# DLRM tower: the last tile in two halves, the layers of the tile before it sooner, and the ids loaded first

## The reference

```
e = jnp.stack([tbl_0[ids[:, 0]], ..., tbl_31[ids[:, 31]]], axis=1)        # [2048, 32, 256]
dots = jnp.einsum('bnd,bmd->bnm', x, x);  z = dots[:, iu, ju]              # pairs i < j, 496 of them
h = jnp.concatenate([z, dense_ctx], axis=1)                                # [2048, 512]
h = jnp.maximum(h @ W_top1 + b_top1, 0.0)                                  # 512
h = jnp.maximum(h @ W_top2 + b_top2, 0.0)                                  # 256
y = h @ W_top3                                                             # [2048, 1]
```

## Time and profile before

| | |
|---|---|
| median of 3 runs | 615.87 us (612.99 to 616.21) |
| the profiled execution | 614.14 us, its span 612.3 us |
| PE, share of the span busy | 85% |
| POOL | 71% |
| DVE, ACT | 45%, 34% |

### The profile page before, as it was taken

The page is one execution under the profiler, slowest core; times in us unless marked ns, Lnnn a source line. Parts: engine busy times, 40 slices in busy tenths (PEclk is TensorE's granted clock), DMA queues, the critical chain, the costliest instruction groups (busy, mean ns, idle before and its releaser), DMA issues.

```text
span 612.3 us, 24786 instructions
## 1 busy us (share of the span) xinstructions
PE 522.7 (85%) x11392; PEld 466.6 (76%) x11392; DVE 278.3 (45%) x600; ACT 209.6 (34%) x390; POOL 432.1 (71%) x463
## 2 busy tenths in 40 slices
PE   1068998999999999988999898989989897996967
PEld 0054796998889897978889786978878796984857
DVE  0013744827364545555273535556263555426060
ACT  1044233343433334343334224333332333432130
POOL 6767677777777777777777777777777777777600
PEclk9978998999999999998999999999999999998788
DMA  5695443443434343433434343434434333333300
GB/s 155 210 241 191 136 139 107 110 126 107 122 111 125 109 121 112 125 107 108 124 110 123 106 126 111 122 107 112 125 105 122 109 109 108 107 108 111 97 3 1
DMA packets 26411, 72.10 MB, mean 118 GB/s; under 512 B 8426, under 2 KB 9338, under 8 KB 25680
## 3 DMA queue, kind: packets, MB, share of 16 engines
q0 software_dynamic: 21888, 59.80, 35.5%
q1 hardware_dynamic: 4420, 10.72, 5.6%
HBM read 70.48 MB, written 0.01 MB: 115 GB/s over the span
## 4 chain that ended last, share of the span: by engine, by line
PE 65%; DMA 14%; POOL 11%; issue 7%; ACT 1%; DVE 1%; SPq 0%; POOLq 0%; ACTq 0%
PE ps_l L268 18%; PE ps_turn L205 15%; POOL rows L192 11%; PE ps_gram L252 11%; DMA rows<-in_table,index 10%; PE ps_pick L234 7%; PE ps_pick L236 7%; DMA pick_id<-in_pick_ids 5%; PE ps_l L279 2%; PE ps_l L220 1%; PE ps_pick L220 1%; PE ps_l L286 1%; DVE pairs L422 0%; PE ps_l L222 0%; PE ps_pick L222 0%
## 5 line engine op out<-in xcount | busy, mean ns | idle before, releaser
L192 POOL DMA_INDIRECT rows<-in_table,index x456 | 431.2, 946 | 146.3 <-issue 118.8
L422 DVE COPY pairs<-ps_gram 32x112 f32<-32x112 f32 (+1 forms) x504 | 189.1, 375 | 140.9 <-PE ps_gram L252 134.5
L327 ACT COPY cols<-ps_turn 128x512 f32<-128x512 f32 x228 | 132.1, 590 | 314.5 <-PE ps_turn L205 314.1
L205 PE MATMUL ps_turn<-identity,rows 128*128 128x128 f32 x912 | 148.2, 293 | 59.0 <-DMA rows<-in_table,index 44.6
L205 PEld LDWEIGHTS ps_turn<-identity,rows 128*128 128x128 f32 x912 | 104.0, 147 | 74.8 <-DMA rows<-in_table,index 41.2
L252 PE MATMUL ps_gram<-cols 128*32 128x32 f32 x8192 | 113.5, 201 | 22.9 <-issue 21.3
L252 PEld LDWEIGHTS ps_gram<-cols 128*32 128x32 f32 x8192 | 93.4, 111 | 49.9 <-issue 44.4
L410 DVE TENSOR_TENSOR one_hot<-ps_ids,row_number 125x2048 fp32r<-125x2048 f32 x28 | 63.9, 2281 | 139.5 <-ACT ps_ids L339 118.9
L268 PE MATMUL ps_l<-pairs,w_sb 128*128 128x128 f32 x1024 | 121.9, 282 | 3.1 <-DVE score L441 3.1
L268 PEld LDWEIGHTS ps_l<-pairs,w_sb 128*128 128x128 f32 x1024 | 120.5, 199 | 3.6 <-DVE pairs L422 3.6
L234 PE MATMUL ps_pick<-one_hot,table_hi 125*128 125x256 f32 x448 | 115.1, 295 | 0.4 <-ACT stage L343 0.4
(11 more groups left out here) (31 smaller groups left out, 79.1 us busy)
## 6 DMA issues: line engine op xcount, KB each, us to landing
rows<-in_table,index POOLq DMA_INDIRECT x456
pick_id<-in_pick_ids SPq DMA_DIRECT2D x14, 250.0 KB
w_sb<-in_w_t SPq DMA_DIRECT2D x1, 2048.0 KB, 29.9
cols<-in_tbl SPq DMA_DIRECT2D x2, 1000.0 KB
stage<-in_tbl SPq DMA_DIRECT2D x2, 1000.0 KB
w_sb<-in_W_top SPq DMA_DIRECT2D x1, 512.0 KB, 32.6
pairs<-in_dense_t SPq DMA_DIRECT2D x16, 8.0 KB
scores<-score SPq DMA_DIRECT2D x16, 0.5 KB
```

Source lines behind the costliest of these rows:

```text
L192: pool.indirect_dma_start(out=rows[x % ROWS][:, k, :], out_offset=None, in_=table, in_offset=bass.IndirectOffsetOnAxis(ap=index[:, t, SUBS ...
L205: last = pe.transpose(ps_turn[x % TURNS][:, h, SPG * k:SPG * (k + 1), :], rows[x % ROWS][:, k, h * P:(h + 1) * P], identity[:, :])
L327: act.copy(cols[t % COLS][:, :, :, FPU * u:FPU * (u + 1)], ps_turn[x % TURNS][:, :, :, :]).then_inc(cols_ready, 1)
L422: last = dve.tensor_copy(pairs[n % 2][N_FIELDS * q:N_FIELDS * (q + 1), c0:KC, TQ * j + FQ * u:TQ * j + FQ * (u + 1)] .rearrange("p c g -> ...
```

## The change

- The ids of the first two picks are loaded ahead of the first two tables.
- In the last two blocks of the loop, t = 30 and 31, `gram_parts` has two parts, at u = 0 and u = 1.
- Tile 14: `layer1` moves from block 31, u = 1 to block 30, u = 5; `relu1` to block 31, u = 0; `layer2` from behind the loop to block 31, u = 2; `layer3` from behind `gram(31)` to block 31, u = 5. Its layers 2 and 3 write the bank of the picks (`ps_late`, a view of `ps_pick`) instead of `ps_l1`. `layer3(13)` moves from u = 4 to u = 2 of block 30.
- Tile 15 is split in halves. Its first half, the 64 samples of block 30, runs `layer1` in block 31 (`first_half_layer1(0)` at u = 4 and `(2)` at u = 5: 32 matmuls of 128 columns of weights by 64 moving columns) and `layer2` right behind `gram(31)`. Its second half, the samples of block 31, runs layers 1 and 2 "column-tiled": each matmul of 128 output rows becomes four of 32, one for each column group of the array, 128 matmuls in layer 1 and 32 in layer 2, 64 moving columns each. The rectifying of the second half's layer 1 is shared by ACT and DVE. Layer 3 and the score run once over all 128 samples.

```diff
...
     def gram_parts(t):
+        if t >= BLOCKS - 2:
+            return {0: (0, FQ // 2), 1: (FQ // 2, FQ)}
         return {2: (0, 4), 3: (4, 8), 4: (8, 12), 5: (12, 16)} if t % 2 == 1 else {1: (0, 6), 2: (6, 11), 3: (11, 16)}

...
+        ps_late = ps_pick[:, :, :].rearrange("p h s -> p (h s)")
+        ps_late_l2 = [ps_late[:, P * m:P * (m + 1)] for m in range(M2C)]
+        ps_late_l3 = ps_late[0:1, 2 * P:3 * P]
+        ps_last_l1 = [ps_l1[:, 0, :], ps_l1[:, 1, :], ps_ids[:, 0:P], ps_ids[:, P:2 * P]]
+        ps_last_l3 = ps_late[0:1, 3 * P:4 * P]
...
+            load_ids(0)
+            load_ids(1)
             load_table(0)
             load_table(1)
-            load_ids(0)
-            load_ids(1)
...
-                if n == TILES - 1:
-                    pe.wait_ge(last_pairs_ready, 1)
...
+                if n == TILES - 2:
...
+                        last = pe.matmul(ps_late_l2[m] if n == TILES - 2 else ps_l1[:, m, :], w2_sb[:, c, m * P:(m + 1) * P],
...
+                    last = pe.matmul(ps_late_l3 if n == TILES - 2 else ps_l1[0:1, M2C, :], w3_sb[:, m:m + 1],
...
+            def last_pairs(c, half):
+                return pairs[(TILES - 1) % 2][:, c, :].rearrange("p (j u g) -> p j u g", j=QUAD, u=2)[:, :, half, :]
+
+            def first_half_layer1(m0):
+                if m0 == 0:
+                    pe.wait_ge(pairs_ready, BLOCKS - 1)
+                    pe.wait_ge(dense_loaded[(TILES - 1) % 2], 16 * TILES // 2)
+                    pe.wait_ge(hidden1_ready, TILES - 1)
+                for m in range(m0, m0 + 2):
+                    for c in range(KC):
+                        last = pe.matmul(ps_last_l1[m][:, 0:BLOCK], w1_sb[:, c, m * P:(m + 1) * P], last_pairs(c, 0),
+                                         start=(c == 0), stop=(c == KC - 1))
+                if m0 == 2:
+                    last.then_inc(l1_done, 1)
...
+            def first_half_layer2():
...
+                for m in range(M2C):
+                    for c in range(M1C):
+                        last = pe.matmul(ps_late_l2[m][:, 0:BLOCK], w2_sb[:, c, m * P:(m + 1) * P],
+                                         hidden1[:, c, 0:BLOCK], start=(c == 0), stop=(c == M1C - 1))
...
+            def second_half_layer1():
+                pe.wait_ge(pairs_ready, BLOCKS)
+                pe.wait_ge(last_pairs_ready, 1)
+                for m in range(M1C):
+                    for c in range(KC):
+                        for j in range(QUAD):
+                            p0 = N_FIELDS * j
+                            last = pe.matmul(ps_last_l1[m][p0:p0 + N_FIELDS, BLOCK:P],
+                                             w1_sb[:, c, m * P + p0:m * P + p0 + N_FIELDS], last_pairs(c, 1),
+                                             start=(c == 0), stop=(c == KC - 1))
+                last.then_inc(l1_done, 1)
+
+            def second_half_layer2():
+                pe.wait_ge(last_hidden1_ready, 2)
+                pe.wait_ge(hidden2_ready, TILES)
...
+                            last = pe.matmul(ps_late_l2[m][p0:p0 + N_FIELDS, BLOCK:P],
+                                             w2_sb[:, c, m * P + p0:m * P + p0 + N_FIELDS], hidden1[:, c, BLOCK:P],
+                                             start=(c == 0), stop=(c == M1C - 1))
+                last.then_inc(l2_done, 1)
...
+            def last_layer3():
...
+                    last = pe.matmul(ps_last_l3, w3_sb[:, m:m + 1], hidden2[:, m, :],
...
-                    if t >= 3 and t % 2 == 1 and u == 1:
+                    if 3 <= t < BLOCKS - 1 and t % 2 == 1 and u == 1:
...
-                    if t >= 4 and t % 2 == 0 and u == 4:
+                    if t >= 4 and t % 2 == 0 and u == (2 if t == BLOCKS - 2 else 4):
...
-            layer2(TILES - 2)
+                    if t == BLOCKS - 2 and u == 5:
+                        layer1(TILES - 2)
+                    if t == BLOCKS - 1 and u == 2:
+                        layer2(TILES - 2)
+                    if t == BLOCKS - 1 and u == 4:
+                        first_half_layer1(0)
+                    if t == BLOCKS - 1 and u == 5:
+                        layer3(TILES - 2)
+                        first_half_layer1(2)
             gram(BLOCKS - 1, 0, FQ)
-            layer3(TILES - 2)
-            layer1(TILES - 1)
-            layer2(TILES - 1)
-            layer3(TILES - 1)
+            first_half_layer2()
+            second_half_layer1()
+            second_half_layer2()
+            last_layer3()
...
-                    if t >= 3 and t % 2 == 1 and u == 3:
+                    if 3 <= t < BLOCKS - 1 and t % 2 == 1 and u == 3:
                         relu1((t - 3) // 2)
+                    if t == BLOCKS - 1 and u == 0:
+                        relu1(TILES - 2)
...
+            act.wait_ge(l1_done, TILES)
+            act.wait_ge(l2_done, TILES - 1)
+            for m in range(M1C):
+                rectified = act.activation(hidden1[:, m, 0:BLOCK], ps_last_l1[m][:, 0:BLOCK], ACT.Relu,
+                                           bias=b1_sb[:, m:m + 1])
+            rectified.then_inc(hidden1_ready, 1)
...
-            relu1(last)
+            act.wait_ge(l1_done, TILES + 1)
+            for m in range(2):
+                rectified = act.activation(hidden1[:, m, BLOCK:P], ps_last_l1[m][:, BLOCK:P], ACT.Relu,
+                                           bias=b1_sb[:, m:m + 1])
+            rectified.then_inc(last_hidden1_ready, 1)
...
+            def relu2_half(half):
+                dve.wait_ge(l2_done, TILES + half)
+                for m in range(M2C):
+                    last = dve.tensor_scalar(hidden2[:, m, BLOCK * half:BLOCK * (half + 1)],
+                                             ps_late_l2[m][:, BLOCK * half:BLOCK * (half + 1)], b2_sb[:, m:m + 1],
+                                             0.0, ALU.add, ALU.max)
+                last.then_inc(hidden2_ready, 1)
...
+                if t % 2 == 0 and 4 <= t < BLOCKS:
                     take_score((t - 4) // 2)
+                if t == BLOCKS - 1:
+                    relu2(TILES - 2)
+                    take_score(TILES - 2)
                 if t % 2 == 0 and t < JOBS:
                     make_one_hot(t)
-            relu2(TILES - 1)
-            take_score(TILES - 1)
+            relu2_half(0)
+            dve.wait_ge(l1_done, TILES + 1)
+            for m in range(2, M1C):
+                last = dve.tensor_scalar(hidden1[:, m, BLOCK:P], ps_last_l1[m][:, BLOCK:P], b1_sb[:, m:m + 1],
+                                         0.0, ALU.add, ALU.max)
+            last.then_inc(last_hidden1_ready, 1)
+            relu2_half(1)
+            dve.wait_ge(l3_done, TILES)
+            dve.wait_ge(stored[(TILES - 1) % 2], 16 * (TILES // 2 - 1))
+            dve.tensor_copy(score[:, (TILES - 1) % 2, :].rearrange("p (j u g) -> p j u g", j=QUAD, u=2),
+                            ps_last_l3.rearrange("p (u j g) -> p j u g", u=2, j=QUAD)).then_inc(score_ready, 1)
...
```

More of the change, by code:

```diff
@@ L285, in layer3 @@
                 for m in range(M2C):
-                    last = pe.matmul(ps_l1[0:1, M2C, :], w3_sb[:, m:m + 1], hidden2[:, m, :],
+                    last = pe.matmul(ps_late_l3 if n == TILES - 2 else ps_l1[0:1, M2C, :], w3_sb[:, m:m + 1],
+                                     hidden2[:, m, :], start=(m == 0), stop=(m == M2C - 1))
+                last.then_inc(l3_done, 1)
+            def last_pairs(c, half):
+                return pairs[(TILES - 1) % 2][:, c, :].rearrange("p (j u g) -> p j u g", j=QUAD, u=2)[:, :, half, :]
@@ new lines, in first_half_layer2 @@
+            def first_half_layer2():
+                pe.wait_ge(hidden1_ready, TILES)
+                pe.wait_ge(score_ready, TILES - 1)
+                for m in range(M2C):
[14 more added lines that the diff above has]
+                last.then_inc(l1_done, 1)
@@ L287, in layer3 @@
+            def last_layer3():
+                pe.wait_ge(hidden2_ready, TILES + 1)
+                for m in range(M2C):
+                    last = pe.matmul(ps_last_l3, w3_sb[:, m:m + 1], hidden2[:, m, :],
                                      start=(m == 0), stop=(m == M2C - 1))
@@ L432, in relu2 @@
                 for m in range(M2C):
-                    last = dve.tensor_scalar(hidden2[:, m, :], ps_l1[:, m, :], b2_sb[:, m:m + 1],
+                    last = dve.tensor_scalar(hidden2[:, m, :], ps_late_l2[m] if n == TILES - 2 else ps_l1[:, m, :], b2_sb[:, m:m + 1],
                                              0.0, ALU.add, ALU.max)
@@ L440, in take_score @@
                     dve.wait_ge(stored[n % 2], 16 * (n // 2))
-                dve.tensor_copy(score[:, n % 2, :], ps_l1[0:1, M2C, :]).then_inc(score_ready, 1)
+                dve.tensor_copy(score[:, n % 2, :], ps_late_l3 if n == TILES - 2 else ps_l1[0:1, M2C, :]
+                                ).then_inc(score_ready, 1)
+            def relu2_half(half):
+                dve.wait_ge(l2_done, TILES + half)
+                for m in range(M2C):
```

(4 more changed lines are left out.)

6 lines of the change are left out of this document (3 added, 3 removed).

## The result

The changed kernel takes 623.42 us (median of 4 runs, 620.12 to 624.65), the kernel before beside it 616.04 us (4 runs, 612.99 to 616.29): a ratio of 1.0129 on record, 95% interval 1.0095 to 1.0163 (the two medians divided give 1.0120). The prediction was 611.5 us, range 606.5 to 615.5, with a chance of 0.08 for slower. It was wrong. The profiled execution's span is 621.2 us, 8.9 longer than before.

What follows compares the result with a forecast made beforehand. POOL paces the middle, a serial chain the end. Start -1.8, start of `gram(31)` +5.9, `gram(31)` -1.2, layer 1 -4.9, layer 2 and small steps -1.8: span 608.45 us, predicted time 611.5, range 606.5 to 615.5.

Steps and rivals of the forecast that it cites:

- The clock term of the first half's layer 1: Lower clock after some 3 us of idle PE adds 1.4 us to that layer's 7.3, bounds 0 and 7.3.
- a clock loss that stays: Rival: lower clock through all of both halves' layer 1 (+5.9, +2.3), 619.7 us; chance 0.05.
- Start: Loading the ids first removes POOL's wait near 33 us: -1.8 us, bounds 0 and 2.1.
- the start gives nothing: Rival: POOL's two later waits grow by what the first one lost, 613.3 us; chance 0.22.
- Up to the first half's layer 1: Tile 14's layer 1, then block 30's dot products and copies, end at 582.3 us, where the first half starts.
- Units and layer 3 between its parts: Two transposes, layer 3 of tile 14 and the last unit's evacuation, ahead of block 31's dot products: 2.0 us together.
- `gram(31)`: The dot products of block 31 take 3.7 us instead of 4.9, bounds 2.8 and 4.9.
- Second half's layer 1: At the end, 256 column-tiled records in groups of four take 5.0 us where 9.92 stood.
- The rest of the end: Around the second half's layer 1: copies 3.43 us and a handover, rectifying 0.6, layer 2 1.4, then the small steps.
- The order's loss: Block 31's dot products start 5.9 us later: 7.3 us of layer 1 stand ahead, only half finding idle time.

Runs made afterwards that it cites:

- e8: The kernel before, with layer 1 of tiles 2 to 15 streaming only 64 of its 128 moving columns: 624.39 us, ratio 1.015.
- e1: The changed kernel, with the first half's layer 1 streaming 128 moving columns instead of 64: 617.6 us, ratio 1.0058.
- e7: The kernel before, with layer 1 of the last tile alone streaming only 64 of its 128 moving columns: 621.74 us, ratio 1.0105.
- e9: The kernel before, with the ids of the picks loaded ahead of the small tables: 613.63 us, ratio 0.9989.
- e3: The changed kernel with the last tile undivided, its layers 1 to 3 run whole behind the last dot products: 614.38 us, ratio 1.0.
- e5: e3 with layer 3 of tile 14 behind the last dot products and tile 15's layer 1 not waiting for tile 14's score: 611.86 us, ratio 0.9945.
- e4: e3 with the tables loaded first and 16 unread matmuls between the last dot products and layer 1 of tile 15: 614.05 us, ratio 0.9984.
- e6: e5 with 12 unread matmuls in PE's wait for the last copies: 608.12 us, ratio 0.9879.
- e11: e6 with 22 more unread matmuls in block 30, ahead of layer 1 of tile 14: 612.14 us, ratio 0.9961.

## Why the prediction was wrong, step by step

Against the forecast's 608.45 us of span stand 621.2:

- *The clock term of the first half's layer 1* failed. I took 7.3 + 1.4 us, with 7.3 as the upper bound of the second term; it was 14.2, so 6.9: +5.5. I had seen that half the moving columns don't shorten the record (e8: 7.26 us for 64), and had put the bound right, but sized the term by how layer 1 of tile 14 recovers, which streams 128. e1 and e7 show that this doesn't carry over to 64. This is the rival that had 0.05, "a clock loss that stays": it priced the dot products at 598.9 and the time at 619.7, with the start's 1.8 still in it. But its reason, the wait ahead of the layer, isn't the one that the runs show: e1 has the same wait, and there the clock comes back.
- *Start*: -1.8 forecast, nothing came in this execution: +1.8. The rival "the start gives nothing" is the nearer one (0.2 us over all traces, see e9), but 1.8 isn't excluded by the times.
- *Up to the first half's layer 1*: it starts at 584.39 instead of 582.3: +2.1. The pieces were near (copies of block 29 from 555.87, layer 1 of tile 14 at 562.38 and in 9.71, copies of 6.06), 0.5 and 0.3 later; the other 1.3 are the transposes and dot products of block 30, 6.2 us instead of 4.9, with a stall of 0.82 in "issue".
- *Units and layer 3 between its parts*: 3.2 us instead of 2.0, since they ran at the low clock as well: +1.2.
- *`gram(31)`*: 5.1 us instead of 3.7, just beyond the upper bound of 4.9: +1.4. The stall (1.36) was there, and the records ran partly at the low clock.
- *Second half's layer 1*: 5.9 instead of 5.0, inside the bounds: +0.9. The rest of the end: -0.3 in rectifying and layer 2, +0.1 in the copies.

Together 12.7, from 608.45 to 621.2. The order's loss, `gram(31)` later because 7.3 us of layer 1 stand ahead of it, was forecast at 5.9 and is in e1 594.15 - 587.11 = 7.0; with the low clock it is 14.7. e3 and e5 show that layer 3 of tile 14 ahead of the last dot products (in e3 together with the wait for its score) takes back some 0.55%, e1 against e3 that the halves as placed cost about as much again. That the useful part of the change is the earlier place of tile 14's layers is what then remains of e5's gain; it wasn't tested apart from the two-part dot products.

The chance was sized badly too. The argument against that rival was a row of 128-column records, and no row of before had a record with 64 moving columns; a term with bounds of 0 and 7.3 us, argued from a row of another shape, deserved more than 0.05.

## What to carry to other kernels

Before you shorten the moving operand of a matmul behind a wait, ask for the clock: if the weight load sets the record's time, the narrow record saves nothing and may hold PE at the lower clock (14.2 us instead of 9.3 or 10.6 here). Work split off the end must fill a wait behind the last dependency, not stand ahead of it. And a wait of some 3 us ahead of a long serial matmul stretch is worth filling with matmuls that nobody reads, as long as they end before the wait does (e4's overran it by 0.8 us, and its ratio is 0.9984 where e3 has 1.0): e6 is 1.2% faster than before for that and for the new order of tile 14 with layer 3 behind the dot products.

## What the runs showed of the hardware that I had not expected

- PE busy without a gap for 13.9 us (e7) and the granted clock at 0.50 to its end, while records of the same weights with 128 moving columns raise it within some 5 us. The Trainium skill ("TensorE: Matmul & The Clock Gate", Part 1) says that the clock returns once the engine has been busy. By that rule e7's layer 1 would have taken the 9.92 us of before; it took 13.89, so a PE that the profile shows as busy was not enough here.
- The stalls in "issue" inside the dot products come in every variant, in those of block 31 1.1 us (e3) to 2.6 us (e9) each, and in e11 twice, with 128 records (256 instructions) between them. The profile of the changed kernel has 92 packets for 1.51 MB of instructions, 16 KB each:

```profile
q8 instruction: 92, 1.51, 1.0%
```

In the traces of the kernel before, the changed one and e11, one such packet moves shortly ahead of each of these stalls: 588.0 to 588.5 before the one at 588.7 (kernel before), 603.5 to 604.0 before 605.0 (changed kernel), 584.5 to 585.0 and 588.0 to 588.5 before 585.4 and 588.4 (e11). That fits a wait for instructions, but it is nearness in time; no run tested it. The stalls' number and place differ between variants that add or take away PE instructions ahead of them, so a difference of 2 us from an edit like that should be looked for there first.
